# Transposes, the attention rows' product, inverse norms and a few VectorE steps at other tiles of the same round, in the last phase of a three-stage decoder block

## The reference

```
x = x + attention(layernorm(x))            # low-rank q and kv, rope, causal softmax, Wout, bout
Q = layernorm(x)
q = l2norm_per_head(layernorm(Q, g1, b1) @ wq)          # 16 heads of 64
k = l2norm_per_head(layernorm(ctx, g1, b1) @ wk);  v = layernorm(ctx, g1, b1) @ wv
y = Q + (q @ k.T @ v) @ wo + bo                         # linear attention, no softmax
y = y + gelu(layernorm(y, g2, b2) @ w1 + b1) @ w2 + b2
x = x + y
x = x + gelu(layernorm(x) @ ternary(W1).T + fb1) @ ternary(W2).T + fb2
```

## Time and profile before

| | |
|---|---|
| timed executions | 1321.4, 1324.18, 1326.83 us |
| the profiled execution's own time | 1330.29 us |
| its span | 1328.3 us |
| mean granted clock of TensorE over the span | 0.904 of full speed |
| last phase, 641 to 1328 us | 687 us; PE busy 597.2, DVE 401.6, ACT 346.7, POOL 148.3 us |
| rounds 2 to 6, from one `z1` transpose to the next | 80.0, 79.8, 83.8, 79.9, 83.9 us |

### The profile page before, as it was taken

The page is one execution under the profiler, slowest core; times in us unless marked ns, Lnnn a source line. Parts: engine busy times, 40 slices in busy tenths (PEclk is TensorE's granted clock), DMA queues, the critical chain, the costliest instruction groups (busy, mean ns, idle before and its releaser), DMA issues. The chain is left out here.

```text
span 1328.3 us, 23288 instructions
## 1 busy us (share of the span) xinstructions
PE 1056.3 (80%) x7133; PEld 770.3 (58%) x7133; DVE 809.3 (61%) x1737; ACT 650.2 (49%) x1155; POOL 371.4 (28%) x516
## 2 busy tenths in 40 slices
PE   3777058798999993895278899898999989898997
PEld 2444023343444441774256778777788777786986
DVE  3888455566777762764355566565576655665544
ACT  1334115565666664463035555473644736346454
POOL 0334226666333331100221222022221212211110
PEclk9777558999999997798579999999999999999999
DMA  3332423333222204146511111112110121000000
GB/s 87 104 118 75 126 92 111 114 102 119 90 87 89 84 27 146 63 199 265 169 47 65 48 64 34 31 63 63 63 49 14 63 63 63 16 25 40 17 1 32
DMA packets 52994, 103.89 MB, mean 78 GB/s; under 512 B 6656, under 2 KB 32768, under 8 KB 48832
## 3 DMA queue, kind: packets, MB, share of 16 engines
q1 hardware_dynamic: 49756, 95.62, 21.4%
q0 software_dynamic: 1920, 6.03, 1.5%
q10 hardware_dynamic: 1252, 1.39, 0.3%
HBM read 63.05 MB, written 39.58 MB: 77 GB/s over the span
## 5 line engine op out<-in xcount | busy, mean ns | idle before, releaser
L803 ACT ACTIVATE p_probs<-p_psS 128x512 f32<-128x512 f32 (+1 forms) x352 | 181.4, 563 | 125.4 <-ACTq L802 122.6
L705 DVE CUSTOM_DVE_ANT_0 p_psA<-p_psA,p_mask 128x512 f32<-128x512 f32 (+1 forms) x256 | 155.7, 647 | 107.3 <-DVEq L703 107.0
L1856 DVE TENSOR_TENSOR p_hl<-p_h,p_hh 128x512 fp32r<-128x512 f32 x128 | 105.7, 829 | 129.1 <-DVEq L1855 128.7
L837 PE MATMUL p_psA<-p_ks,p_qs 96*128 96x512 bf16 (+3 forms) x512 | 145.0, 319 | 36.0 <-PEq L835 35.5
L1674 ACT ACTIVATE p_h<-p_psG,w_columns 128x512 f32<-128x512 f32 x128 | 88.1, 689 | 149.8 <-ACTq L1673 149.7
L856 PE MATMUL p_psS<-p_qs,p_ks 99*128 99x256 bf16 (+3 forms) x512 | 131.8, 311 | 20.2 <-PEq L881 11.7
L2127 PE MATMUL p_psY<-p_n,p_hh 128*128 128x256 f32 x512 | 106.8, 292 | 18.8 <-PEq L2118 16.7
L724 POOL TENSOR_SCALAR_AFFINE_SELECT p_probs<-p_probs 128x512 f32<-128x512 f32 x128 | 80.7, 634 | 133.9 <-POOLq L723 115.4
L867 PE MATMUL p_psO<-p_probs,p_v 128*32 128x512 f32 (+3 forms) x1024 | 93.3, 459 | 27.8 <-PEq L863 27.1
L856 PEld LDWEIGHTS p_psS<-p_qs,p_ks 99*128 99x128 bf16 x512 | 43.9, 98 | 107.1 <-issue 92.4
L2127 PEld LDWEIGHTS p_psY<-p_n,p_hh 128*128 128x128 f32 x512 | 86.1, 196 | 26.8 <-issue 25.6
(11 more groups left out here) (260 smaller groups left out, 2778.2 us busy)
## 6 DMA issues: line engine op xcount, KB each, us to landing
p_n<-n_parts SPq DMA_DIRECT2D x16, 1024.0 KB, 6.8
o_sums<-p_o SPq DMA_DIRECT2D x32, 256.0 KB, 3.0
n_parts<-p_nh SPq DMA_DIRECT2D x8, 1024.0 KB, 3.9
n_parts<-p_nl SPq DMA_DIRECT2D x8, 1024.0 KB, 6.0
q_parts<-p_part SPq DMA_DIRECT2D x48, 128.0 KB
p_qs<-q_parts SPq DMA_DIRECT2D x32, 192.0 KB
p_x<-in_x_dram SPq DMA_DIRECT2D x8, 512.0 KB, 4.5
p_qs<-q_parts SPq DMA_DIRECT2D x32, 128.0 KB
```

Of the source, the lines that this page charges most:

```text
L705: nc.vector.tensor_tensor_reduce(out=bank[:, 0:w], in0=bank[:, 0:w], in1=mask[:, S - w:S], scale=1.0, scalar=MASKED, op0=ALU.add, op1=ALU.max,
L803: nc.scalar.activation(probs[:, g % 2, at:at + n * w], psS[place(s, turn) % SB][:, 0:n * w], ACT.Exp, scale=SCALE).then_inc(exp_done, 1)
L837: last = nc.tensor.matmul(bank[:, z * w:(z + 1) * w], qs[0:SROWS, k, g * G + r0 + z, i * P:(i + 1) * P], ks[0:SROWS, k, g, 0:w], start=Tru ...
L1856: nc.vector.tensor_tensor(hl[:, s, :], h[:, s, :], hh[:, s, :].bitcast(F32), ALU.subtract).then_inc(h_parts, 1)
```

## The change

No instruction of arithmetic is added or taken away. Steps stand at other tiles:

| step | engine | before | now |
|---|---|---|---|
| `z3` transposes | PE, ACT | behind query 2 and 4 | behind query 3 and 5 |
| `z2` second transpose | PE, ACT | behind ternary 3 | behind ternary 5 |
| `z1` first transpose | PE | behind finish m3 (before m6) | behind begin m6 |
| `z1` second remainder (`affine_low`) | DVE | at the end of MLP | at cross 1 |
| `inverses`, `norm_blocks`, rounds 2 to 6 | DVE | at ternary 3 and 4 | at MLP 3 and 5; the PSUM pair is still given back at ternary 3 (`norms_taken`) |
| `z2` second remainder | DVE | at ternary 5 | at ternary 6 |
| `o_high`, `o_low` (parts of the attention rows' operand) | DVE | at ternary 5 and 6 | at ternary 3 and 4 |
| `output_rows` | DVE | behind the remainder of m1 | ahead of it |
| `prepare_o` | DVE | round 1: ahead of `cross_rows` | behind `z2` |
| `attention_rows`, round 0 | PE | before CROSS | behind query 6; its sum on DVE ahead of the inverses |
| `norms`, round 1 | ACT, DVE | at MLP 1 | at MLP 0 |
| `q0_rows`, last round | DVE | at ternary 7 | at cross 2 |

The diff, cut to its core:

```diff
                 for m in range(XT):
                     query(m)
-                    if m == 2:
+                    if m == 3:
                         plain(th, 0)
-                    if m == 4:
+                    if m == 5:
                         plain(th, 1)
                 for m in range(XT):
...
                         affine(bh, w["ln2_g"], w["ln2_b"], 0)
-                    if m == 3:
+                    if m == 5:
                         affine(bh, w["ln2_g"], w["ln2_b"], 1)
 
             def mlp(second):
                 for m in range(XT):
                     gelu(w["b1"], place(MLP, m), m)
-                    if m == 1 and second:
+                    if m == 0 and second:
...
                 dve.sem_inc(h_ready, -1)
                 nc.vector.tensor_tensor(hl[:, s, :], h[:, s, :], hh[:, s, :].bitcast(F32), ALU.subtract).then_inc(h_parts, 1)
 
-            def inverses():
+            def norms_taken():
                 dve.wait_ge(norm_ready, 1)
                 dve.sem_inc(norm_ready, -1)
                 nc.vector.engine_nop().then_inc(pair_free[S_PAIR], 1)
+
+            def inverses():
                 stepped(nc.vector.tensor_scalar(n2[:, :], n2[:, :], 1e-12, None, ALU.max))
                 stepped(nc.vector.reciprocal(n2[:, :], n2[:, :]))
...
                 prepare_o()
+                attention_added(False)
+                norms_taken()
                 inverses()
                 norm_blocks()
-                attention_added(False)
                 for m in range(XT):
                     cross(CROSS, m)
-                    if m == 3:
+                    if m == 1:
                         z1()
                     if m == 6:
                         affine_low(fl, fh, 0)
...
             def round_1():
-                prepare_o()
                 cross_rows(CROSS)
                 z2()
+                prepare_o()
                 for c in range(C):
                     affine_low(bl, bh, c)
                 q0_rows(False)
                 for m in range(XT):
                     hidden(place(MLP, m))
-                    if m == 1:
-                        inverses()
-                        norm_blocks()
+                    if m == 0:
+                        norms_taken()
                     mlp(m)
-                for m in range(XT):
-                    cross(CROSS, m)
+                cross_with_feature()
 
             def queries_and_ternary(more):
 
...
                         affine_low(bl, bh, 0)
                     if m == 3:
-                        inverses()
-                    if m == 4:
-                        norm_blocks()
-                    if m == 5:
-                        affine_low(bl, bh, 1)
+                        norms_taken()
                         if more:
                             o_high()
-                    if more and m == 6:
-                        o_low()
-                    if m == 7:
+                        else:
+                            inverses()
+                    if m == 4:
+                        if more:
+                            o_low()
+                        else:
+                            norm_blocks()
+                    if m == 6:
+                        affine_low(bl, bh, 1)
+                    if more and m == 7:
                         q0_rows(False)
 
             def mlp(m):
                 if m == 2:
                     attention_added(False)
+                if m == 3:
+                    inverses()
                 if m == 4:
                     z1()
-                if m == 6:
+                if m == 5:
+                    norm_blocks()
+                if m == 7:
                     affine_low(fl, fh, 0)
-                if m == 7:
-                    affine_low(fl, fh, 1)
+
+            def cross_with_feature():
+                for m in range(XT):
+                    cross(CROSS, m)
+                    if m == 1:
+                        affine_low(fl, fh, 1)
 
             def round_():
                 queries_and_ternary(True)
                 for m in range(XT):
-                    hidden(place(MLP, m))
                     if m == 1:
                         output_rows(TERNARY, x2)
+                    hidden(place(MLP, m))
                     mlp(m)
-                for m in range(XT):
-                    cross(CROSS, m)
+                cross_with_feature()
 
             def last_round():
                 queries_and_ternary(False)
                 for m in range(XT):
                     cross(LAST_CROSS, m)
+                    if m == 2:
+                        q0_rows(False)
                 output_rows(TERNARY, x2)
...
 
-            BEGUN = {("query", 2): 0, ("query", 4): 1, ("ternary", 1): 0, ("ternary", 3): 1,
+            BEGUN = {("query", 3): 0, ("query", 5): 1, ("ternary", 1): 0, ("ternary", 5): 1, ("mlp", 6): 0,
                      ("ternary 6", 5): 0, ("ternary 6", 7): 1}
-            BEGUN_1 = {("query", 4): 0, ("query", 6): 1}
-            FINISHED = {("mlp", 3): 0, ("mlp", 5): 1, ("mlp 6", 2): 0, ("mlp 6", 4): 1, ("mlp 7", 2): 0, ("mlp 7", 4): 1}
+            BEGUN_1 = {("query", 4): 0, ("query", 6): 1, ("mlp", 6): 0}
+            FINISHED = {("mlp", 5): 1, ("mlp 6", 2): 0, ("mlp 6", 4): 1, ("mlp 7", 2): 0, ("mlp 7", 4): 1}
             FINISHED_0 = {("cross", 3): 0, ("cross", 5): 1}
...
                 for stage in stages:
-                    if stage is CROSS and len(stages) == len(ROUND_0):
-                        attention_rows()
...
                         held.append((stage, m))
+                        if stage is QUERY and len(stages) == len(ROUND_0) and m == 6:
+                            attention_rows()
                         transposes(begun, (stage.name, m))
                 while len(held) > (0 if drain else LAG):
```

## The result

The changed kernel takes 1288.97 us (median of four, 1285.26 to 1291.85) against 1325.51 of the kernel before on the same chip: a ratio of 0.9721, 95% interval 0.969 to 0.9751. The forecast was 1287.

What follows compares the result with a forecast made beforehand. PE's queue was taken to set the loop's time. Savings of 20.5 + 8.0 + 11.5 + 1.9 = 41.9 us from the profiled 1330.3 gave 1288.4, or 1282; forecast 1287 us, own range 1279 to 1295, full range 1276 to 1304.

Steps and rivals of the forecast that it cites:

- Wait for `z3`: Loop round, PE's wait of 0.76 us for z3: goes and nothing replaces it, a gain of 0.75.
- TERNARY: Loop round, PE's 2.12 us wait for psT: split into about 1.6 and 0.9, MLP's first tile later, a loss of 0.75.
- Attention rows: Loop round, PE's 1.29 us wait for output_rows before the attention rows: goes fully, a gain of 1.45.
- `z1`: Loop round, PE's 1.82 us wait for z1: a wait of 0.6 is left, a gain of 1.2 to 1.4.
- CROSS: Loop round, PE's wait before the first row product of CROSS: 0.35 us instead of 1.51, a gain of 1.15.
- Round: One loop round: the savings on its waits, plus 0.1 to 0.3 for closer products, sum to about 4.1 us.
- 20.5 + 8.0: The five loop rounds: 20.5 us from about 4.1 a round, plus 8.0 because the two longer rounds cannot return.
- 84 us shape: Two of five loop rounds took 4 us more, both remainders m0 and m1 behind both adds: can't return, -8.0, bound 0.
- Rounds 0 and 1: The phase's first two rounds: 3.2 + 3.9 + 2.5 + 1.9, a gain of 11.5 us, bounds 7 and 15.
- half of a clock fall of 3 us: Round 1, after its first finish: half of a 3 us clock fall is saved, the 1.9 term.
- Last round and tail: Last round: z3 wait and low clock go, 3.25 before CROSS becomes two waits of together 2.6: -1.9, bounds 0 and -4.
- first rival: Clock and adds, 18%: TERNARY's split waits drop the clock, m0's remainder waits behind both adds, 3.3 a round: 1303 us.

Runs made afterwards that it cites:

- z2_transpose_at_5_alone: The kernel before with only the second z2 transpose moved behind ternary 5 and its remainder to ternary 6: 1333.0 us (ratio 1.0044).
- output_first_alone: The kernel before with only output_rows moved ahead of m1's remainder: 1314.25 us (ratio 0.989).
- z2_transpose_at_3: The changed kernel with the second z2 transpose and ACT's affine back behind ternary 3, the remainder left at 6: 1289.02 us (ratio 0.9691).
- loop_only: The changed kernel with rounds 0 and 1 as before, except round 1's z1 transpose and second z1 remainder, which stay changed: 1291.87 us (ratio 0.974).
- first_rounds: The kernel before with rounds 0 and 1 alone changed, without round 1's z1 transpose and second z1 remainder: 1325.13 us (ratio 0.9983).
- small_adds: The changed kernel with POOL's q0 and x1b adds cut to 4 columns instead of 1024, bo and b2 left out elsewhere: 1283.96 us (ratio 0.9663).
- z1_transpose_at_m3: The changed kernel with the first z1 transpose back ahead of m6, behind finish m3, in rounds 1 to 6: 1300.72 us (ratio 0.98).

## Why the prediction was right

Point by point, forecast and measured:

- *Wait for `z3`*: 0 forecast, 0 measured.
- *TERNARY*: 1.6, 0.9 and less than 1.3 before m0 forecast; 1.58, 0.68 and 0.63 measured.
- *Attention rows*: wait gone, m0's remainder "about 2 us" forecast; 1.90 measured.
- *`z1`*: 0.6 forecast, 0.34 measured. *CROSS*: 0.35 forecast; 0.24 measured, too short to be listed above.
- *Round*: 79.84 - 4.1 = 75.7 forecast, 75.50 measured. The five rounds took 407.5 us before (first CROSS row products, 765.32 to 1172.78) and take 377.5 now: 30.0 less, where 20.5 + 8.0 = 28.5 was forecast. Both terms came from the right places. z2_transpose_at_5_alone has the 84 us shape's wait in every round with m1's remainder ahead of `output_rows`; output_first_alone and z2_transpose_at_3 have the order reversed and do not have it in any round, though the clock fell in some. What the prediction did not see is that a fall alone does not make such a round, as the first loop round before shows.
- *Rounds 0 and 1*: 11.5 forecast, 123.47 - 113.62 = 9.85 measured. The shortfall of 1.65 is less than the 4.3 us by which these rounds scatter when nothing in them is changed, so the total does not show the term mis-sized. The rows show three flaws. I missed the new wait of 0.78 for the last squares. I had the first row product of CROSS about 2.2 earlier, when it came only 1.5 earlier in the phase (50.24 to 48.77 us from its start). And the 1.9 for "half of a clock fall of 3 us" has no source in the rows: from the first row product of MLP to the `z1` transpose the kernel before took 16.29 us (737.25 to 753.54) and z2_transpose_at_5_alone, without the fall, 14.76, so the whole fall cost 1.5, and all of it went. The steps of their own were given 3.2 + 3.9 + 1.9 = 9.0; loop_only puts them at 6.7.
- *Last round and tail*: 1.9 forecast, 41.4 - 30.0 - 9.85 = 1.6 left over; the waits of 1.74 and 0.90 are the "two waits of together 2.6". The terms that the prediction names there come to 0.7 + 3.25 - 2.6 + 1.6 = 2.95 and not to 1.9; the wait of 1.07 that stayed before the first row product, and that it does not name, is the difference.

That the sum was met to 0.5 us is in part luck: the loop gave 1.5 more than forecast, rounds 0 and 1 gave 1.65 less, and the last round 0.3 less.

The median came out at 1289 and not 1287. The profiled execution before had been 6.1 above its median; I guessed that this was 84 us rounds that the others lacked. Nothing bears that out: first_rounds, with more such rounds, had no longer a median, and the start of the phase alone scatters by 11 us over the profiles. That guess stays open.

Half of the first rival's mechanism is real: both adds do stand ahead of m0 and m1. The other half, a fall of the clock behind the split waits, came in no round. And where a fall did come, in z2_transpose_at_3, the rival's price was still not paid: `output_rows` had its place ahead of m1's remainder, and the attention rows did not wait. The Trainium skill, "SBUF — State Buffer", section "SBUF: two separate sides", says that a VectorE instruction with two SBUF inputs and a GpSimd instruction lock each other out of a shared port pair, and that the one that starts first keeps it to its end. The traces agree: every stretched remainder ends 0.54 to 0.56 after an add. small_adds shows that the stretch costs nothing in the loop, where PE comes back later than that.

## What to carry to other kernels

When one engine sets the time, list its waits in one round, and for each ask what is late next; a moved step is worth its wait less the next one, and here that sum held to 0.2 us a round. Parts of such a change don't add: one of them alone made the kernel slower and is harmless only beside another, and a gain in front of a loop with two round lengths was, by one profile, half given back by the loop. Where two engines contend, a round's length can hang on which of two instructions starts first, here by 0.01 to 0.03 us. After an edit, the next candidate is the engine that released the longest wait left; here it was ACT's two table loads, and moving them to the stage where ACT had idle time before every tile gave 2.7 us a round, as much as the `z1` transpose and the second `z1` remainder together (1.4 and 1.3).

## What the runs showed of the hardware

A wait of 2.12 to 2.14 us brought PE's clock to the 1.2 GHz level in some rounds and not in others of the same program: in the first, third and fifth loop round of the kernel before and of first_rounds, in three of five rounds of z2_transpose_at_3, in the first two of output_first_alone. The two waits of 1.58 and 0.68, which stand 2.8 us apart, never did in any loop round of the changed kernel. Two falls followed shorter waits, 1.82 in output_first_alone (at 1153.25) and 1.76 in the last round of z1_transpose_at_m3 (at 1198.46), where such waits elsewhere did nothing. The low level cost about 1.4 us where it was not followed by a wait for the adds (76.0 against 74.6).

A 128x512 remainder on DVE that met a 128x1024 add on POOL took up to 2.94 us instead of 0.69, and the order of their starts decided it, down to 0.03 us. And the three phases that no kernel here changed differed by up to 10.8 us from one profile to the next, more than most of the parts under study.
